# A fused FFT-convolution, mixture-of-experts and scan kernel: half 0 alone goes forth and back, with block 0 stacked

## Time and profile before

| | |
|---|---|
| median of 3 runs | 329.05 us (327.38 to 330.6) |
| profiled execution, its own time | 326.64 us |
| its span in the trace | 324.5 us |
| busy PE, DVE, ACT, POOL | 280.3, 241.4, 150.6, 130.0 us |
| mean granted TensorE clock | 0.954 of full speed |

### The profile page before, as it was taken

One profiled execution on the slowest core, in us unless ns is written; L12 is line 12 of the kernel. 1 busy time (PEld: TensorE's weight loads), 2 busy tenths in 40 slices (PEclk: granted clock), 3 DMA queues, 4 the chain that ended last, 5 costly groups with the idle time before them and its releaser, 6 DMA issues.

```text
span 324.5 us, 3788 instructions
## 1 busy us (share of the span) xinstructions
PE 280.3 (86%) x1016; PEld 164.3 (51%) x1016; DVE 241.4 (74%) x570; ACT 150.6 (46%) x512; POOL 130.0 (40%) x205
## 2 busy tenths in 40 slices
PE   0799840898998789969999999999999999999991
PEld 0688730766774336435654654565455445444340
DVE  2898997497889986989598769858886773874600
ACT  1217462329343267744656376546735641642222
POOL 3769404636000032148666745775574210110111
PEclk9999955679799999999999999999999999999998
DMA  6991000005746200191019105700950392095111
GB/s 216 313 348 38 0 2 0 0 1 207 316 172 249 102 1 1 62 421 40 0 32 421 71 1 202 319 1 6 356 195 2 132 393 60 19 401 169 33 32 32
DMA packets 19429, 43.55 MB, mean 134 GB/s; under 512 B 2256, under 2 KB 14544, under 8 KB 15184
## 3 DMA queue, kind: packets, MB, share of 16 engines
q1 hardware_dynamic: 18016, 41.57, 34.7%
q10 hardware_dynamic: 1264, 1.74, 1.6%
q0 software_dynamic: 128, 0.00, 0.0%
HBM read 40.95 MB, written 2.36 MB: 133 GB/s over the span
## 4 chain that ended last, share of the span: by engine, by line
issue 31%; POOL 23%; DVE 21%; PE 16%; ACT 4%; DMA 3%; SPq 1%; POOLq 0%; ACTq 0%; DVEq 0%
PE ps L374 5%; PE ps L468 3%; POOL rs L847 3%; DVE third L1196 3%; DMA xy<-in_L_attn_x 3%; POOL second L878 2%; POOL second L873 2%; POOL second L866 2%; POOL second L874 2%; POOL rs L856 2%; ACT tok L584 2%; POOL second L867 2%; PE ps L423 2%; DVE stats L1099 1%; POOL ve L852 1%
## 5 line engine op out<-in xcount | busy, mean ns | idle before, releaser
L468 PE MATMUL ps<-third,w_out 128*128 128x512 f32 x256 | 115.1, 592 | 0.0
L468 PEld LDWEIGHTS ps<-third,w_out 128*128 128x128 f32 x256 | 47.2, 190 | 54.5 <-issue 47.2
L1196 DVE TENSOR_TENSOR third<-ps,first 128x512 f32<-128x512 f32 x120 | 73.4, 680 | 0.3
L607 ACT ACTIVATE first<-ps 128x512 f32<-128x512 f32 x32 | 19.1, 597 | 34.9 <-PE ps L440 21.2
L843 POOL TENSOR_TENSOR ve<-ssq,eps 128x4 f32<-128x4 f32 x16 | 3.2, 199 | 78.3 <-ACT xy L639 61.0
L374 PE MATMUL ps<-second,third 128*128 128x256 f32 x96 | 28.6, 458 | 4.1 <-DVE second L986 4.1
L1205 DVE TENSOR_TENSOR second<-ps,xT 128x512 f32<-128x512 f32 x16 | 10.9, 682 | 22.1 <-PE ps L468 22.1
L374 PEld LDWEIGHTS ps<-second,third 128*128 128x128 f32 x96 | 21.6, 231 | 9.7 <-issue 5.9
L834 POOL TENSOR_TENSOR ve_<-vr_,eps 128x8 f32<-128x8 f32 x4 | 0.9, 232 | 57.9 <-DVE vr_ L1110 57.9
L374 PE MATMUL ps<-first,third 128*128 128x256 f32 x96 | 21.3, 380 | 0.7 <-DVE first L986 0.7
L1223 DVE TENSOR_TENSOR_SCAN second<-col,second 128x512 f32<-128x512 f32 x16 | 20.7, 1336 | 1.5 <-POOL second L866 1.5
(11 more groups left out here) (266 smaller groups left out, 519.7 us busy)
## 6 DMA issues: line engine op xcount, KB each, us to landing
first<-gates SPq DMA_DIRECT2D x32, 1024.0 KB, 6.8
xy<-in_L_attn_x SPq DMA_DIRECT2D x16, 128.0 KB, 7.0
out<-xy SPq DMA_DIRECT2D x8, 256.0 KB, 3.2
third<-in_fwd ACTq DMA_DIRECT2D x3, 512.0 KB, 6.7
third<-in_inv SPq DMA_DIRECT2D x1, 1536.0 KB, 7.6
w_out<-in_L_ffn_w SPq DMA_DIRECT2D x2, 512.0 KB, 6.1
third<-in_L_attn_t SPq DMA_DIRECT2D x1, 256.0 KB, 5.4
w_sin<-in_L_ffn_w_shared_in SPq DMA_DIRECT2D x2, 128.0 KB, 5.7
```

Of the source, the lines that this page charges most:

```text
L468: last_ = mm(y_ps[:], w_out[l][:, 1 + e], hs[(EXPERTS * n + e) % 16], start=False, stop=(e == EXPERTS - 1))
L607: run(sil[kind], gate_ps[:], ACT.Silu).then_inc(silu_done, 1)
L1196: tt(hs[(EXPERTS * n + e) % 16], rows[:], wbc[n % 2][:, e], MUL).then_inc(scaled, 1)
```

## The change

- Block order 3 1 5 2 4 0 instead of 1 5 3 2 4 0. The forward sums of a half are cut into 4 pieces instead of 6 (6, 9, 7 and 6 operations), the filter's sums into 3 (3, 6 and 8), and they alternate: filter 0 and 1, x 0 and 1, filter 2, x 2, first products, x 3.
- Half 1's forward sums: one piece (6 operations) ahead of half 0's inverse and none inside it; the other three pieces come behind `moments1(0)`.
- Block 0: cosine and sine of k1 = 0 are stacked side by side in one matrix, and those of k1 = 6 in another. The forward turn of block 0 has 2 matmuls instead of 4, its inverse turn takes the products directly (4 matmuls; POOL's sums for this block are dropped in both halves), the filter's block 0 is kept by one copy on ACT, and `keep_filter0` and `bin0` are dropped.
- x is loaded by SP (batches 0 and 2) and ACT (batches 1 and 3), two chunks of one batch in each DMA, half 0's first. The forward matrices of blocks 1 and 3 stay first on ACT's queue; those of 2 and 5, then 0 and 4 go to SP's queue behind its half of x of half 0.
- PE starts with 8 matmuls of 128x256 on zeros (`keep_running`), which only need a DVE memset.
- The norm: DVE makes `ve1` with one more small operation, POOL has one fewer (2 instead of 3).
- Table steps 4 to 7 move on ACT and DVE, and the routing of batch 0 and 1 is interleaved in another way.

The diff, cut to its core:

```diff
-ORDER = [1, 5, 3, 2, 4, 0]
+ORDER = [3, 1, 5, 2, 4, 0]
...
+    c0, s0, c6, s6 = np.cos(at0), np.sin(at0), np.cos(at6), np.sin(at6)
+    s0[:, 0] = np.cos(np.pi * n2[:, 0])
+    m[0] = np.hstack([c0, s0]), np.hstack([s0, c0]), np.hstack([c6, s6]), np.hstack([s6, c6])
...
+PAIRS = [(0, 6), (2, 2), (1, 4), (3, 4)]
...
+        T_KEPT = 2 * (BLOCKS - 1) + 1
+        def spectra_after(half, i):
+            return 2 * ((BLOCKS - 1) * half + i + 1)
...
-                for n in (0, 6, 2, 4, 1, 5, 3, 7):
-                    sp.dma_start(y_all[:, n, b:b + 2], x_dram[:, n, b:b + 2]).then_inc(x_loaded[half][n], 16)
+                for i, (n, step) in enumerate(PAIRS):
+                    sp.dma_start(y_all[:, n:n + step + 1:step, b], x_dram[:, n:n + step + 1:step, b]).then_inc(
+                        x_loaded[half][i], 16)
+                if half == 0:
+                    sp.dma_start(fwd[:, 2:6:3], d["fwd"][:, 2:6:3]).then_inc(fwd_loaded[1], 16)
+                    sp.dma_start(fwd[:, 0:5:4], d["fwd"][:, 0:5:4]).then_inc(fwd_loaded[2], 16)
...
                 k = ORDER[i]
+                pe.wait_ge(dve_t, after(T_DVE, T_READY[k]))
...
-                    pe.wait_ge(spectra, 2 * (6 * half + i + 1))
+                    if k:
+                        pe.wait_ge(spectra, spectra_after(half, i))
+                    else:
+                        pe.wait_ge(products, 2 * (6 * half + i + 1))
...
+                    if k == 0 and kind == "f":
+                        last_ = mm(target, fwd[:, 0, 2 * o, :], source[o], start=True, stop=True)
+                        continue
                     for q in range(2):
...
+                        rows = prod[i % 2][q][:, o * HALF:(o + 1) * HALF] if k == 0 else source[q]
+                        last_ = mm(target, matrix[:, k, 2 * o + q, :], rows, start=(q == 0), stop=(q == 1))
...
-            pe.wait_ge(dve_t, len(T_DVE))
-            for i in range(4):
-                pe.wait_ge(fwd_loaded[i // 2], 16)
-                filter_block(i)
-            transform_block(0)
+            def keep_running(count):
+                for _ in range(count):
+                    mm(to_ch[:, 0:HALF], idle_rows[:, 0:P], idle_rows, start=True, stop=True)
+            pe.wait_ge(rows_set, 1)
+            keep_running(8)
+            pe.wait_ge(fwd_loaded[0], 16)
+            filter_block(0)
+            filter_block(1)
+            pe.wait_ge(fwd_loaded[1], 16)
+            filter_block(2)
+            for turn in range(3):
+                transform_block(turn)
+            filter_block(3)
             pe.wait_ge(fwd_loaded[2], 16)
             filter_block(4)
-            transform_block(1)
             filter_block(5)
-            for turn in range(2, 6):
+            for turn in range(3, 6):
                 transform_block(turn)
...
-            act.dma_start(fwd[:, 1:6:4], d["fwd"][:, 1:6:4]).then_inc(fwd_loaded[0], 16)
-            act.dma_start(fwd[:, 2:4], d["fwd"][:, 2:4]).then_inc(fwd_loaded[1], 16)
-            act.dma_start(fwd[:, 0:5:4], d["fwd"][:, 0:5:4]).then_inc(fwd_loaded[2], 16)
-            act.dma_start(bin0[:], d["bin0"]).then_inc(const_loaded, 16)
+            act.dma_start(fwd[:, 1:4:2], d["fwd"][:, 1:4:2]).then_inc(fwd_loaded[0], 16)
+            for b in (1, 3):
+                for i, (n, step) in enumerate(PAIRS):
+                    act.dma_start(y_all[:, n:n + step + 1:step, b], x_dram[:, n:n + step + 1:step, b]).then_inc(
+                        x_loaded[b // 2][i], 16)
...
+                if k == 0:
+                    run(t_spec[:, 0:4], t_ps[i % 2][:].rearrange("p (a c) -> p a c", a=4), ACT.Copy).then_inc(t_kept, 1)
+                    return
...
             silu(0, 1)
-            table_products(4)
             copy_gates(0)
             normalise1(2)
-            table_products(5)
             normalise1(3)
             copy_channels(1, 2)
+            copy_channels(1, 3)
+            table_products(4)
+            table_products(5)
+            exponentials(1)
             table_products(6)
-            copy_channels(1, 3)
-            exponentials(1)
-            table_products(7)
             keep_inverse(18)
             keep_inverse(19)
             silu(1, 0)
             keep_inverse(20)
             copy_gates(1)
             silu(1, 1)
+            table_products(7)
...
-                tt(ve1[:, b], vr1[:, b], eps[:], ADD).then_inc(pool_ln1, 1)
-                pool.wait_ge(pool_ln1, b * 3 + 1)
                 tt(rs1[:, b], ve1[:, b], half_neg[:], ALU.pow).then_inc(pool_ln1, 1)
...
                 if piece == 0:
-                    have(0, 6)
+                    have(0)
                     tt(d06, x[0], x[6], SUB).then_inc(step, 1)
-                    tt(E, x[0], x[6], ADD).then_inc(step, 1)
-                    have(2, 4)
+                    have(1)
                     tt(d24, x[2], x[4], SUB).then_inc(step, 1)
-                    tt(D, x[2], x[4], ADD).then_inc(step, 1)
-                    have(1, 5)
+                    have(2)
                     tt(s15, x[1], x[5], ADD).then_inc(step, 1)
+                    have(3)
+                    own("s15")
+                    tt(H, s15, x[7], SUB).then_inc(step, 1)
+                    tt(v[3][0], d06, d24, SUB).then_inc(step, 1)
+                    own("H")
+                    tt(v[3][1], H, x[3], SUB).then_inc(step, 1)
...
-            filter_sums()
-            for piece in range(6):
-                forward_transform(0, piece)
-            for i in range(3):
-                multiply_spectra(0, i)
-            keep_filter0()
-            for i in range(3, 6):
+            nc.vector.memset(idle_rows, 0.0).then_inc(rows_set, 1)
+            filter_sums(0)
+            filter_sums(1)
+            forward_transform(0, 0)
+            forward_transform(0, 1)
+            filter_sums(2)
+            forward_transform(0, 2)
+            multiply_spectra(0, 0)
+            forward_transform(0, 3)
+            for i in range(1, 6):
                 multiply_spectra(0, i)
             set_rank()
-            for piece in range(3):
-                forward_transform(1, piece)
+            forward_transform(1, 0)
             inverse_transform(0, 0)
-            forward_transform(1, 3)
             inverse_transform(0, 1)
             moments1(0)
             multiply_spectra(1, 0)
-            forward_transform(1, 4)
+            forward_transform(1, 1)
+            forward_transform(1, 2)
             multiply_spectra(1, 1)
             moments1(1)
-            forward_transform(1, 5)
+            route_first(0)
+            forward_transform(1, 3)
+            multiply_spectra(1, 2)
+            route_second(0)
             table_sums(3)
-            route_first(0)
-            route_second(0)
-            multiply_spectra(1, 2)
+            hidden(0)
             multiply_spectra(1, 3)
-            hidden(0)
+            multiply_spectra(1, 4)
             table_sums(4)
-            multiply_spectra(1, 4)
+            multiply_spectra(1, 5)
             table_sums(5)
-            multiply_spectra(1, 5)
             route_first(1)
             route_second(1)
             table_sums(6)
             scale_rows(0, {})
+            hidden(1)
             table_sums(7)
-            hidden(1)
             inverse_transform(1, 0)
```

More of the change, by code:

```diff
@@ L224, in build @@
         gates = nc.dram_tensor("gates", (ROUTES, 2 * EXPERTS * TILES, P), F32).ap()
-        x_loaded = [[sem(f"x_loaded{h}_{n}") for n in range(CHUNKS)] for h in range(2)]
+        x_loaded = [[sem(f"x_loaded{h}_{n}") for n in range(CHUNKS // 2)] for h in range(2)]
         t_loaded, param_loaded = sem("t_loaded"), sem("param_loaded")
@@ L716, in slot @@
                     factor_products()
-            for i in range(BLOCKS - 1):
+            for i in range(BLOCKS):
                 keep_filter(i)
@@ L895, in _ @@
                 square_power(j)
-            for i in range(BLOCKS):
+            for i in range(BLOCKS - 1):
                 product_sums(0, i)
-                if 4 + i < DOUBLINGS - 1:
-                    square_power(4 + i)
+            for j in range(4, DOUBLINGS - 1):
+                square_power(j)
             scale_shift1(0)
@@ L905, in _ @@
             scale_shift1(1)
-            for i in range(2, BLOCKS):
+            for i in range(2, BLOCKS - 1):
                 product_sums(1, i)
@@ L950, in forward_transform, with have @@
                 v = u[half]
-                def have(*chunks):
-                    for n in chunks:
-                        dve.wait_ge(x_loaded[half][n], 16)
+                def have(pair):
+                    dve.wait_ge(x_loaded[half][pair], 16 * 2)
                 def own(name):
@@ L980, in forward_transform @@
                     stt(v[5][0], B, -ROOT, A, MUL, ADD).then_inc(step, 1)
-                    own("H")
-                    stt(C, H, 0.5, x[3], MUL, ADD).then_inc(step, 1)
-                    tt(G, d15, x[7], ADD).then_inc(step, 1)
-                if piece == 3:
```

(3 more changed lines are left out.)

159 lines of the change are left out of this document (73 added, 86 removed).

## The result

The changed kernel took 323.74 us in the median of four runs (322.45 to 325.48), beside 329.13 for the kernel before in the same job: ratio 0.985, with a 95% interval of 0.9813 to 0.9886. Measured again in five rounds it was 323.96 us, 0.9872 [0.9824, 0.9921]. By the ratios it is 4.2 to 4.9 us faster, by the medians 5.4 in both; 322.7 us, a gain of 6.3, was forecast.

The account below looks back on a forecast made before the run. Slots bound by PE; the front by PE to 39.52 us, DVE to 56.9, then short steps. Statistics 6.0 plus POOL 0.3, plus 0.5, less 0.7, gives 6.1; `scale_shift1` makes 6.3: 329.05 to 322.7 us, range 318.5 to 327.

Parts of the forecast that it names:

- Loads: Start of the kernel: half 0's x there at 10.6 us, matrices 2 and 5 landed at 12.6.
- Rival 1: Loads: transfers don't come earlier, turn 0 stays at 16.7 us, total about 325 us; chance 0.15.
- Half 0's turns: PE in the front: turn 0 at 13.7 us, then 23.2 us to 36.9 instead of 39.52; gain taken as 2.8.
- the ring of products: DVE's products feeding PE's turns 4 to 8: closest margin 0.1 us at turn 6, up to 1 us may be lost.
- The inverse and the statistics: DVE after half 0's turns: statistics done at 46.5 us instead of 52.5, gain 6.0; POOL's dropped operation 0.3 more.
- The moved sums: Half 1's forward sums behind the statistics: hidden by the norm with nothing to spare; uncovered they cost 3.1 us.
- The tables: Table steps on ACT and DVE: 0.5 us gained at batch 1's logits, routing some 0.7 us later through DVE's wait.
- Rival 3: Between ACT and DVE: tables, moved sums or routing lose the gain, leaving 2.5 us, about 326.5 us; chance 0.13.
- The same pattern, moved: PE's clock: half-clock stretches as before but shifted; two later ones worth 1.7 us each, bound 3.4 us either way.
- more than 7 us at half clock between 60 and 90: Sign that would show the forecast wrong: a clock row at 0.5 between 60 and 90 us for over 7 us.
- Rival 2: PE's clock stays at 1.2 GHz until the slots begin: +13 - 6.3, or 335.7 us; chance 0.06.
- can only slide: The slots, 112 to 300 us: same in both kernels, bound by PE and its neighbours' pattern; nothing taken off for the tail.

Follow-up runs that it names:

- experiment 1: The changed kernel again with no edit, its second measurement and profile: 323.96 us, 0.9872 of the kernel before.
- Experiment 11: Changed kernel with number 8's edits plus idle matmuls in the wait for matrices 2 and 5 and ahead of batch 1's second transposes and logits: 319.40 us, 0.9698.
- experiment 4: Changed kernel with its loads as before (x all on SP, the forward matrices on ACT): 325.14 us, 0.9884 of the kernel before.
- Experiment 3: Changed kernel with half 1's forward sums put back ahead of and inside half 0's inverse: 326.77 us, 0.9927 of the kernel before.
- Experiment 6: Changed kernel with table steps and routing of batches 0 and 1 in the old order on ACT and DVE: 325.57 us, 0.992 of the kernel before.
- experiments 2: Changed kernel without the 8 idle matmuls at its start: 323.16 us, 0.9834 of the kernel before.
- experiment 10: Number 8's kernel without the 8 idle matmuls at the start: 320.18 us, 0.9727 of the kernel before.
- experiment 12: The kernel before with idle matmuls in all its PE gaps, the waits of slots 1 and 3 included: 325.34 us, 0.99 of the kernel before.
- number 9: Changed kernel with the place of half 1's sums, the loads, block 0's work and the table and routing order all put back: 330.56 us, 1.0032.
- number 8: Changed kernel with 26 idle matmuls behind turn 12 and 4 in each of PE's waits in slots 1 and 3: 321.71 us, 0.9794.

## Why the prediction was right, and where it was off

The time came out 1.0 us above the forecast, well inside the range; the terms of the sum were off by more than that, and partly cancel: half 0's turns came 1.7 us late, the tables brought some 2 us more than put, and the slots took 2.6 us longer in both profiles. That the sum came so near is in part luck.

**Loads.** Turn 0 was put at 13.7 us and started at 13.97. x was put at 10.6 and was there at 11.34, the matrices at 12.6 and PE was released at 12.91. Rival 1 (the transfers don't come earlier) is out: with the old loads x is there at 14.07. In the second profile turn 0 started at 14.86 (experiment 1).

**Half 0's turns, the step that failed.** The sum gave 23.2 us from turn 0 to the end of turn 11, so 36.9 us, and took a gain of 2.8 (39.52 - 36.9 is 2.6). Measured: 38.6, a gain of 0.9. Two terms were too small, and they came out equally late.

The first is PE's own. All twelve turns were priced at 1.74 us, full clock. Behind the wait for the matrices the clock was at half from 13.8 to 17.2 us, and turns 0 to 2 took 6.8 us (13.97 to 20.77) instead of 5.2. So turn 5 ended at 28.0.

The second is the ring of products, where "up to 1 us may be lost" was too small: the products of turn 3, whose bank turn 6 takes, end at 28.0 instead of 26.3. Three things made DVE late. x came 0.7 later than put, and the first products start at 19.48 (19.0 in the sum). Then DVE's six sums (the last forward piece) took 3.15 us (20.68 to 23.83) instead of 2.0: the two that run beside POOL's product sums took 0.94 us each instead of 0.41. And the pair at 26.66 waits 0.43 us for POOL. The trace of the kernel before already had such a price, beside POOL's addition from 34.33:

```profile
34.58 0.94 DVE L974 TENSOR_TENSOR second<-second,xy 128x256 f32<-128x256 f32 x1
```

Turn 6 starts at 28.05, when both are done. Experiment 11 takes the first away: turns 0 to 2 are 1.6 us faster and turn 6 is not earlier, so DVE's products hold it there. In other profiles PE alone is late: in the second one of the changed kernel turn 6 starts at 28.95 with the products of turn 3 done at 28.01, in experiment 4 at 30.60 with them done at 29.6. The sign named for the ring, gaps between turns 3 and 8, does not show in the changed kernel, where PE has no wait there; it shows in experiment 11, at 23.01 and 25.12. No run takes away DVE's lateness alone.

**The inverse and the statistics.** The chain is as forecast, 1.8 us late: first inverse part at 34.19 (32.4 forecast), second wait 37.65 (35.9), statistics' last operation 48.26 (46.5). Each step keeps its distance to PE's turns, so nothing further failed there. The gain is 4.4 us at POOL's square root (52.87 to 48.51; 49.34 in the second profile), 6.3 was forecast with POOL's own 0.3. ACT's norm starts at 50.73 (48.9 forecast).

**The moved sums** were to be covered with nothing to spare. They are: block 1's sums end at 52.6 on DVE, and PE, which waits for ACT's norm till 52.52, takes turn 13 at 53.40. Experiment 3 gives their place 1.8 to 2.5 us. By its middle value it is the largest of the parts, but the tables' is the same within the error.

**The tables, a term of the wrong sign.** I put 0.5 gained against 0.7 lost. DVE does wait 2.64 us for ACT at 75.00, as the list of signs named, but nothing on the path waits for DVE then: the logits it needs come from PE at 77.7. By the trace the freed ACT is what counts. Experiment 6 gives 1.6 to 2.3 us, of which 1.3 show at the logits of batch 1. I had priced the visible wait of DVE and not asked whether the logits would end later anyway.

**Block 0** was put at 0.4 + 0.5 us and measured at 0.7 to 1.4; **`keep_running`** at nothing, and is nothing (experiments 2 and 10).

**The sum of the parts.** Against the mean of the two measurements of the changed kernel (0.9861), one part undone costs 2.2 us (sums), 0.8 (loads), 1.1 (block 0) and 1.9 (tables), 6.0 together; all four undone cost 5.6. So the parts add up, each with about 1.5 us of error. Rival 3 (the gain lost between ACT and DVE) is out by this: both of its places were gains.

**The clock, and slots that did not only slide.** "The same pattern, moved" was nearly right for the front. At half clock in the first profile were 13.7, 3.4 and 6.8 us between 44 and 82 (20.4, 3.4 and 3.5 before). At 75.3 the logits of batch 1 took 3.05 us; in experiment 11 they took 1.94. The sign "more than 7 us at half clock between 60 and 90" was met there, at 10.2 us; in the second profile only 3.4 us (76 to 80) lay between 60 and 90. Rival 2 is thus a true mechanism, at the size of its pieces and not of its 13 us.

What the prediction had wrong is that the slots "can only slide", with nothing taken off for the tail. Both profiles of the changed kernel have 3.4 us at half clock in slot 1 and again in slot 3 (at 109.4 and 143.5 in the first), with PE busy throughout. From the first `add_input` to the end it was 215.8 and 215.9 us in these two, 213.2 in the kernel before, and with the gaps filled 213.0 (experiment 11) and 213.3 (experiment 12). So the first `add_input` came 3.4 and 4.9 us earlier (6.1 forecast), and 0.8 and 2.2 were left in the spans. The profiled execution of before was a fast one; whether its slower runs have such stretches is not on record, but low time over its runs, 26.7 to 37.5 us, overlaps with 30.8 to 40.4 in the changed kernel.

The price of the half clock by the medians is 4.3 us in the changed kernel (experiment 11) and 3.6 in the kernel before (experiment 12 against 328.92 in the same job). The difference, 0.5 to 0.8 us (1.7 to 2.4 by the ratios), would be what of the gain the clock took; it is not clear of the error.

The Trainium skill's "TensorE: Matmul & The Clock Gate", section "HAM oscillation — how this bites in real kernels", holds that gaps between bursts of matmuls bring the half clock back each time. The runs agree in part: with the gaps filled, low time falls from 31 to 40 us to 4.4 to 7.0. They do not agree on "each time": behind the same waits in slots 1 and 3 the kernel before stayed at full clock in its profile (last section).

**Left open.** What the loads are worth: experiment 4 is 0.4 to 1.1 us slower by the ratios. Its profile, set beside the changed kernel's second one, which was taken in the same job, is 1.7 us later all along: the last record of turn 10 ends at 39.40 instead of 37.75, the logits of batch 1 start at 76.48 instead of 74.83, `add_input` at 108.07 instead of 106.40, and the span is 324.0 instead of 322.3. The 2.5 us at the turns are against the first profile, so 0.9 of them is the spread of one kernel. Whether the new block order or the cut of the sums costs the 0 to 1.4 us that number 9 shows was not tried. And idle matmuls at the start seem to cost 1.5 us beside those of number 8: low time is higher with them (experiment 10), but why it is was not shown.

## What to carry to other kernels

- When one engine of a ring starts earlier, work out the other engines' times too, and price each at the clock and beside the neighbours that it will have. Here PE started 2.8 us earlier and kept 0.9 of it: it ran its first turns at half clock, and without that DVE's products would have held it up just as long.
- A wait that appears on an engine costs only if its successor on the chain is waited for; compare its end with the time when the next input would be there anyway.
- Where TensorE idles ahead of work on the path, try matmuls into a free bank: they brought 4.3 us here, and the spread of the runs fell from 3 us to 0.4. Those at the very start, ahead of a wait of 3.4 us, brought nothing.

## What the runs showed of the hardware

- Elementwise operations of 128 x 256 in float32 took 0.94 us on DVE instead of 0.41 while POOL ran its additions of the same size beside them (0.84 to 0.90 instead of 0.73). It can fall on the other engine: in experiment 4 DVE's six sums kept 0.42 each, and POOL's addition beside them took 2.52 us.
- The spread of this kernel's runs goes with the clock. The changed kernel with 30.8 us of low time had a span of 320.7 us, with 36.9 one of 323.7; with the gaps filled, six runs lay within 0.41 us.
- A wait does not always bring the half clock. In the changed kernel's first profile PE waits 2.25 us in slot 1 (until 108.62) and 3.00 in slot 3 (until 142.80), and the half clock sets in 0.8 and 0.7 us after it is busy again. The kernel before has the same two waits, 2.25 us until 112.01 (below) and 3.01 until 145.29, and its clock stays at 1.00 behind both (112 to 300 us in the earlier trace rows):

```profile
112.01 0.66 PE L402 MATMUL ps<-ident,second 128*128 128x128 f32 x4 [2.25 <-DVE second L1205]
```

Idle matmuls in these waits take the half clock away:

```profile
110.00:300.00 190.00, 185.45 (x653) 97.60 (x651) 144.17 (x291) 100.52 (x343) 81.15 (x85) 1.00 0.37 143
```
```profile
110.00:300.00 190.00, 184.10 (x639) 96.28 (x639) 143.36 (x296) 100.49 (x344) 82.37 (x86) 0.98 0.37 141
```

The first line is experiment 11, the second the changed kernel: 190 us at clock 1.00 and at 0.98.
